# Convolution stage of a two-layer kernel: sixteen pair sums ahead of the transposes, six of them on GpSimd

## What is computed

```
enh  = depthwise3x3(conv1x1(x))
h    = grouped3x3(x); h1, h2 = halves of h
attn = conv1x1(h1 * h2) * attgamma + conv1x1(x)             # 16 rows per pixel
attk = attn @ selfw                                         # per pixel: 2 x 18 numbers for each of 64 channel pairs
y    = sum over 18 (2 channels x 9 taps) of attk * (enh moved by the tap) + attn @ selfb
out  = y * ga1 + enh + x
```

## Time and profile before

| | |
|---|---|
| median of 3 runs | 5619.45 us (5618.39 to 5619.49) |
| the profiled execution | 5617.04 us, its span 5615.3 us |
| granted TensorE clock, mean | 0.993 |
| busy by the page: TensorE, VectorE, ScalarE, GpSimd | 5483.5, 5154.6, 3475.7, 4337.8 us |
| layer 0 | to about 1920 us |
| convolution stage | from about 1920 us, 64 bands |

### The profile page before, as it was taken

How to read it: one execution, slowest core, us unless ns; L and a number is a source line. 1 busy time by engine, 2 the same in 40 slices (tenths; PEclk the granted TensorE clock), 3 DMA queues, 4 the chain that set the end, 5 groups by cost and what they waited for, 6 DMA issues and landing times.

```text
span 5615.3 us, 113386 instructions
## 1 busy us (share of the span) xinstructions
PE 5483.5 (98%) x38408; PEld 3959.2 (71%) x38408; DVE 5154.6 (92%) x5413; ACT 3475.7 (62%) x4284; POOL 4337.8 (77%) x1895
## 2 busy tenths in 40 slices
PE   8999999999999799999999999999999999999998
PEld 7888888888887366666666666666666666666666
DVE  7888888888888499999999999999999999999999
ACT  6888888888887455555555555555555555555553
POOL 4655555555565688889888888888888888888885
PEclk9999999999999799999999999999999999999999
DMA  3222222222221122222222222222222222222221
GB/s 89 75 75 75 75 75 75 75 75 75 74 74 58 57 69 73 70 73 63 76 64 67 74 68 72 65 77 62 72 68 68 74 68 72 64 78 61 68 72 44
DMA packets 155247, 394.18 MB, mean 70 GB/s; under 512 B 35136, under 2 KB 38400, under 8 KB 155136
## 3 DMA queue, kind: packets, MB, share of 16 engines
q1 hardware_dynamic: 155200, 393.56, 22.9%
HBM read 219.37 MB, written 136.31 MB: 63 GB/s over the span
## 4 chain that ended last, share of the span: by engine, by line
PE 48%; DVE 13%; issue 4%; POOL 1%; DVEq 0%; ACT 0%; POOLq 0%
PE ps_k L975 18%; PE ps_t L992 15%; DVE products L1159 9%; PE ps_m L958 7%; PE ps_p L945 4%; DVE products L1165 2%; PE ps_t L1000 1%; DVE ps_k L1159 1%; PE ps_t L1009 1%; POOL enh L911 1%; PE ps_m L965 1%; PE ps_t L1007 1%; DVE h_prod L1179 0%; DVEq L113 0%; DVEq L1152 0%
## 5 line engine op out<-in xcount | busy, mean ns | idle before, releaser
L911 POOL TENSOR_TENSOR enh<-enh,tap 128x1280 f32<-128x1280 f32 (+1 forms) x1024 | 2515.7, 2457 | 115.3 <-ACT tap L1108 61.6
L1159 DVE TENSOR_TENSOR products<-ps_k,enh 128x1024 f32<-128x1024 f32 x1664 | 1993.6, 1217 | 93.5 <-PE ps_k L975 79.2
L975 PE MATMUL ps_k<-att,basis 128*128 128x512 f32 x4608 | 1697.7, 454 | 59.5 <-DVE products L1165 16.9
L1108 ACT ACTIVATE tap<-e,dw 128x1280 f32<-128x1280 f32 (+1 forms) x1024 | 1250.0, 1252 | 219.5 <-POOL enh L911 219.4
L975 PEld LDWEIGHTS ps_k<-att,basis 128*128 128x128 f32 x4608 | 715.3, 190 | 805.8 <-DVE products L1159 499.5
L470 POOL TENSOR_TENSOR hidden_lo<-hidden,hidden_hi 128x1024 fp32r<-128x1024 f32 x256 | 694.6, 2734 | 730.3 <-DVE hidden_hi L681 730.3
L917 POOL TENSOR_TENSOR products<-products 128x1024 f32<-128x1024 f32 x320 | 765.9, 2393 | 357.6 <-DVE products L1159 357.4
L1159 DVE TENSOR_TENSOR ps_k<-ps_k,enh 128x1024 f32<-128x1024 f32 x640 | 785.4, 1227 | 41.3 <-PE ps_k L975 30.3
L992 PE MATMUL ps_t<-ident_swap,products 128*128 128x128 f32 x5376 | 806.9, 273 | 0.0
L992 PE MATMUL ps_t<-ident,products 128*128 128x128 f32 x5376 | 805.5, 272 | 0.5 <-DVE products L1165 0.5
L1165 DVE TENSOR_TENSOR products<-ps_k,products 128x1024 f32<-128x1024 f32 x640 | 782.8, 1223 | 19.8
(11 more groups left out here) (117 smaller groups left out, 7363.4 us busy)
## 6 DMA issues: line engine op xcount, KB each, us to landing
xin<-layer_out SPq DMA_DIRECT2D x64, 1280.0 KB, 7.3
xt<-in_x SPq DMA_DIRECT2D x128, 512.0 KB, 4.1
layer_out<-xo SPq DMA_DIRECT2D x128, 512.0 KB, 2.9
x_own<-layer_out SPq DMA_DIRECT2D x128, 512.0 KB, 3.9
out<-out_sb SPq DMA_DIRECT2D x256, 256.0 KB, 2.0
att<-att_hi SPq DMA_DIRECT2D x512, 32.0 KB, 2.0
att<-att_lo SPq DMA_DIRECT2D x512, 32.0 KB, 2.0
h_up<-h_sb SPq DMA_DIRECT2D x256, 16.0 KB
```

The costliest lines, as they stand in the source:

```text
L911: nc.gpsimd.tensor_tensor(own, own, tap_sb[add % TAP_BUFFERS][:, 0:hi - lo, :], ALU.add).then_inc(dw_done, 1)
L975: mm = nc.tensor.matmul(ps_k[KERNEL_BUFFER[q]][:, BANK * s:BANK * (s + 1)], basis[:, 2 * t + s, :], att[p][:, j, :], start=True, stop=True)
L1108: nc.scalar.activation(tap_sb[add % TAP_BUFFERS][:, 0:hi - lo, :], src, ACT.Copy, scale=dw[:, t:t + 1]).then_inc(tap_ready, 1)
L1159: nc.vector.tensor_tensor(out, kernels, enh[p][:, r:r + CHUNK_ROWS, dx:dx + W].unsqueeze(1).to_broadcast([C, 2, CHUNK_ROWS, W]), ALU.mult) ...
```

## The change

It alters tables only. `VECTOR_MERGES` (ten) and `POOL_MERGES` (five, now six) name the first product of each pair; the sums of GpSimd now stand at products 0, 4, 13, 20, 24, 29, and VectorE's last four at 22, 27, 31, 33. All functions stay as they are. What follows from the tables: 36 - 16 = 20 terms a band; 46 slots and 13 places as before.

```
-VECTOR_MERGES = (2, 6, 9, 11, 15, 18, 24, 27, 29, 33)
-POOL_MERGES = (0, 4, 13, 21, 31)
+VECTOR_MERGES = (2, 6, 9, 11, 15, 18, 22, 27, 31, 33)
+POOL_MERGES = (0, 4, 13, 20, 24, 29)
...
-TERM_SLOT = {0: 11, 3: 6, 4: 16, 7: 11, 8: 10, 10: 13, 12: 18, 13: 23, 16: 23, 17: 24, 19: 26, 20: 30, 21: 33, 23: 31, 25: 33, 26: 35, 28: 39, 30: 45, 31: 47, 34: 44, 35: 48}
+TERM_SLOT = {0: 7, 3: 6, 4: 11, 7: 11, 8: 12, 10: 19, 12: 16, 13: 25, 16: 23, 17: 22, 19: 27, 20: 31, 23: 32, 24: 38, 26: 35, 28: 39, 29: 44, 32: 43, 34: 47, 35: 47}
...
-BACK_SLOTS = [21, 32, 40, 52]
+BACK_SLOTS = [23, 34, 40, 51]
...
-POOL_MERGE_PLACES = [0.6000000000000001, 1.6, 4.5, 8.0, 13.9]
+POOL_MERGE_PLACES = (0, 1.6, 4.5, 8.0, 10.5, 12.9)
...
-TAP_PLACES = ((0.0, 0.0, 0.0, 1.5, 7.0, 10.0, 12.5, 13.5, 16.0), (22.0, 22.5, 23.0, 26.5, 31.5, 32.5, 35.0, 36.5, 37.5))
-CLEAR_PLACES = [27, 60]
+TAP_PLACES = ((2.0, 2.0, 6.0, 7.0, 10.0, 14.0, 14.5, 15.5, 20.0), (24.0, 24.5, 26.0, 26.5, 31.0, 36.5, 37.0, 38.5, 40.5))
+CLEAR_PLACES = [25, 62]
...
-H_PROD_SLOT = 26
-ATT_HIGH = 26
-ATT_LOW = 35
-CONV_SLOTS = [37, 37, 41, 41, 41, 41, 46, 46, 50, 50, 54, 54, 59, 59, 60, 60, 66, 66]
+H_PROD_SLOT = 27
+ATT_HIGH = 28
+ATT_LOW = 32
+CONV_SLOTS = [34, 34, 41, 41, 41, 41, 46, 46, 50, 50, 54, 54, 59, 59, 60, 60, 66, 66]
 COEFFICIENT_SLOT = 28
-PW_SLOTS = [17, 19, 25, 30, 36]
+PW_SLOTS = [17, 19, 26, 30, 36]
```

## The result

The changed kernel takes 5591.7 us (median of 5 runs, 5591.45 to 5592.97), the kernel before, timed beside it, 5618.39 us; the ratio is 0.9955, interval 0.9944 to 0.9966. It is faster, by 26.7 us between medians; the forecast was 44. That is inside the stated range of 5528 to 5625 us, and just outside the part of it that had the chance of 0.70 (5546 to 5590 us). The profiled execution took 5592.69 us, 24.35 us less than that of before, its span 5591.0. (Lines of the convolution stage stand 6 further down: 975 is now 981, 992 is 998, 1159 is 1165, 1165 is 1171.

What follows compares the result with a forecast made beforehand. VectorE and TensorE, neither full, were taken as tied by two kernel buffers. Waits cut by 0.68 us x 63 bands = 43, plus 1.5 at the end: 44 us off 5617.04, 5573 us; range 5528 to 5625.

Steps and rivals of the forecast that it cites:

- What counts is the bunching, then the sum: TensorE work between two kernels makes VectorE wait if longer than VectorE's slots there; bunching counts first, then TensorE's total.
- gap sums: Per gap between kernels: TensorE's work less VectorE's slot time, excess carried; waits 2.73 us a band before, 2.05 after.
- The new places, by gaps: Waits over VectorE's slots in the new order, kernel pair priced 0.49 us: 0.68 us less per band.
- VectorE: its own work changes by 0: VectorE keeps ten sums, 46 slots and 36 products per band, so its own work changes by 0.
- One term fewer: 20 terms instead of 21: TensorE loses eight transposes, 0.87 us per band, 56 us over 64 bands.
- GpSimd fits: One more GpSimd sum gives 53.3 us of work per band and still fits, with 0.8 us to spare.
- the walk: GpSimd's new order timed from band start: last addition ends at 59.0 us, terms covered 1 to 5 us, least sum 4.
- GpSimd does not slow VectorE: More GpSimd work does not lengthen VectorE's instructions: cost 0, at most 0.04 us a band.
- The end: After VectorE's last slot two terms on TensorE's queue instead of four: some 1.5 us less.
- A: Rival: chunk 2's hand-back in slot 40 comes too late, TensorE stands 1.75 us a band; 5684 us, chance 0.13.
- B: Rival: VectorE is the bound and new bunches take up the removed waits; no change, 5617 us, chance 0.08.
- C: Rival: nearly all VectorE waits go until GpSimd's loop holds, 55.95 us a band; 5518 us, chance 0.09.

Runs made afterwards that it cites:

- old_six: Kernel before plus a sixth GpSimd sum (product 17 added to the sum of 15 and 16), terms 16, 19 and one hand-back moved; 5635.4 us, 1.0037.
- five_sums: Changed kernel without GpSimd's sixth sum (products 29 and 30), so 21 terms a band, all new places kept; 5626.3 us, 1.0018.
- cut_tight: Kernel before with terms 4 (slot 16) and 30 (slot 45) cut to their last transpose each, timing only; 5590.9 us, 0.9956.
- cut_loose: Kernel before with terms 20, 21, 23, 25 (slots 30 to 33) cut to their last transpose each, timing only; 5621.4 us, 1.0008.
- cut_ten: Kernel before with term 10 (slot 13) cut to two of its eight transposes, timing only; 5613.8 us, 0.9993.
- order1: Changed kernel with other slots for terms, hand-backs and grouped taps, picked by the gap sums for least VectorE waits; 5577.5 us, 0.9931.
- old_att34: Kernel before with ATT_LOW = 34 instead of 35, putting att_lo one slot earlier, ahead of a product; 5652.0 us, 1.0060.
- order3: Changed kernel with a third order of the sixteen sums, its slots picked by the refitted gap sums; 5598.8 us, 0.9969.

## Why the prediction was right, and where it was off

**What counts is the bunching, then the sum** held. Slot 17 starts without a wait, and slots 0, 1 and 15 wait in its place, as forecast. Work of 3.05 us removed in slots 30 to 33 gained nothing, 1.5 us in slots 16 and 45 gained 0.38 us a band, and `old_six` lost 0.27 with one term fewer. The gap sums with 0.1 us more for kernels beside grouped taps gave, against measured, in us a band (the 0.1 was set after the first two rows were known; the other rows were worked out before their runs, that of `cut_ten` as 0.0 to 0.1 us less than before):

| kernel | gap sums | measured |
|---|---|---|
| before | 57.55 | 57.56 |
| changed | 57.06 | 57.20 |
| five_sums | 57.66 | 57.74 |
| cut_tight | 57.06 | 57.18 |
| cut_loose | 57.55 | 57.56 |
| cut_ten | 57.54 | 57.50 |
| order1 | 56.39 | 57.01 |

They are good to 0.15 us around the two orders whose traces I had, and 0.6 us too hopeful for an order that was chosen because they liked it.

**The size**: 22 us of the 24 lie in 63 bands x 0.35 us, against 0.68 forecast. The step that was mis-sized is "The new places, by gaps", in two ways. First, it took one price of 0.49 us for every kernel pair. From start to start a pair takes 0.55 us where a term follows and 0.65 where grouped taps follow, as these rows of the changed kernel show and as the earlier trace rows did (3020.81 to 3021.46):

```profile
3007.27 0.72 PE L981 MATMUL ps_k<-att,basis 128*128 128x512 f32 x2
3007.92 1.94 PE L964 MATMUL ps_m<-xin,gT 128*32 128x512 f32 x16
...
3011.15 0.72 PE L981 MATMUL ps_k<-att,basis 128*128 128x512 f32 x2
3011.70 0.60 PE L998 MATMUL ps_t<-ident,products 128*128 128x128 f32 x4
```

With 0.1 us more beside grouped taps the sums give 0.49 us less a band instead of 0.68, and the waits did fall by 0.50 (0.47 with the sum behind att_lo counted rightly). No run varies this price by itself. Second, "VectorE: its own work changes by 0" was wrong by 0.12 us: I took 0.12 off for every one of ten sums before, though that of slot 36 had att_lo ahead of it. The change moved att_lo to slot 32, in front of a product. 0.47 - 0.12 = 0.35 us, what the measured band lost. `old_att34` shows the 0.12 in the kernel before, beside a larger part.

**One term fewer** was sized at 0.87 us of TensorE's time; of that 0.35 to 0.54 us reached the band. **GpSimd fits** held: 53.21 us busy against 53.3 walked, its first addition still released by ScalarE (0.79 us), sum 13 by VectorE (0.63 us). Only the margin was too small: not 0.8 us, since the walk counted the wait before the first addition alone, while in the band from 3011.79 waits of 1.85 us before the fifth and 0.63 before sum 13 take up a late start as well; 1.9 us more cost nothing. That sum 4 had the least cover was right. **GpSimd does not slow VectorE** held at 1209 to 1228 ns. **The end**: from VectorE's last start to the end of the span it was 9.0 us and became 8.3; I had given 1.5 us. "Now two" was wrong: four terms are still on the queue there, since terms 32 and 29 stand behind the last kernel.

**The rivals.** A did not happen: chunk 2's hand-back follows without a wait, 0.5 us after ScalarE's copy ends. (Its price was read from the earlier trace rows, which show the closing of chunk 0, not of chunk 1.) B did not hold, but half of it was right, since 0.5 us of the 0.87 came back as TensorE waits: its idle time before kernels, from 2200 to 5500 us, rose from 34.0 to 61.6 us. The Trainium skill (Perfetto Trace Analysis, Identifying the Most-Contended Engine) would have read VectorE as the bound and TensorE with a third in hand; `cut_loose` agrees, `cut_tight` does not, since VectorE's gaps end on TensorE only at some places. C was never near: `order1`, the best of the runs, still has 2.26 us of waits.

What stays open: why the gap sums miss 0.6 us in `order1` and 0.8 in `order3` (1.84 us of waits by the sums, 2.6 by VectorE's starts). Both have waits of 0.10 us at slot 38 and 0.27 at slot 42 that the changed kernel lacks; no run takes them apart. Open too is how far below 57.0 us a band can go with these two buffers.

## What to carry to other kernels

Where two engines are tied by a double buffer, price a piece of work by the wait that ends behind it, slot by slot, and not by its length: 0.76 us of the same kind of work was worth 0.28 us a band at one place, 0.10 at another and 0 at four more. Follow what stands next in line before you book a removed wait, and look at the queues (here SyncE's store ahead of a load) and at small ops that hide a dependency for free. A model that ranks changes near a measured order does not rank orders that it picked itself: run them.

## What the runs showed of the hardware that I had not expected

A VectorE product starts 1.13 us after the op before it, a sum that reads the product just made 1.25 us after; an independent op of 0.66 us put between them makes that 0.12 us vanish. That the 0.12 us belong to the reading, and not to a sum as such, is shown by the sum behind att_lo, which starts as a product does there, 0.66 us after. A GpSimd addition of 128 x 1024 float32 whose two inputs and output are one and the same region took 1.90 us; the tap additions of that size, with two tiles as inputs, took 2.21 us, and the pair sums 2.40 us. What makes the difference between the three no run isolates.
